# One more group's terms folded on GpSimd, and the routing steps of two groups one slot later

## The chip, the cores and the metric

The kernel runs on one core of a Trainium2 chip. The metric is the device time of one execution in microseconds (us), the median of several runs. TensorE is called PE here, VectorE DVE, ScalarE ACT, GpSimd POOL and SyncE SP in the rows of the profile; each works through its own list of instructions in order, and semaphores are the only thing that ties one list to another.

## The reference

```python
def xattn(k, v, q, ssm_kernel, D, head_dim):          # called with ctx, ctx, layernorm(x)
    kv = jnp.einsum('bhil,bhjl->bijhl', k_, v_)        # k_, v_, q_: [16, 16 heads, 8, 256]
    y = causal_convolution(kv, ssm_kernel)             # written with an FFT of 512
    out = y + kv * D[None, None, None, :, None]
    return jnp.einsum('bijhl,bhil->bjhl', out, q_)     # reshaped to [16, 128, 256]

def moe(x, Wg, W1, W3, W2, sw1, sw3, sw2):             # x: 2048 tokens of 256, E = 8, C = 256
    probs = softmax(xt @ Wg); eidx = argmax(probs); gate = probs[eidx]
    pos = (jnp.cumsum(oh, axis=0) * oh).sum(-1) - 1    # place of a token in its expert's list
    keep = pos < C
    xd = zeros(E * C, d).at[flat].set(xt, mode='drop')
    h = silu(xd @ W1) * (xd @ W3)                      # hidden size 352, per expert
    out = take(h @ W2, flat) * (gate * keep)[:, None]
    shared = silu(xt @ sw1) * (xt @ sw3) @ sw2
    return out + shared

x = x + tanh(g_xattn[0]) * xattn(ctx, ctx, layernorm(x))
x = x + tanh(g_ffn[0]) * moe(layernorm(x))
```

## The kernel before, in words

The 16 batches are worked on in 4 groups (g = 0 to 3) of 4 batches. A group's convolutions take 8 *slots*, one for each pair of heads, so slots 0 to 31 (CONV = 32) hold the convolutions, and slots 32 to 50 the rest of the shared feed-forward; the eight experts follow. Slot s of group g is s = 8g + i. The code is written out by hand: every engine runs `for s in range(SLOTS)`, and the table STEPS says in which slot of the next group a step of group g is due (`due(step, s)`); THIRD_STEPS and LAST_STEPS replace it for groups 2 and 3. Within a slot each engine's order is that of the code.

- GpSimd makes kv, the products of the context (L442 and L445, `kv_products`), eight slots ahead, one for every second slot, in a ring of 5. PE convolves them with Toeplitz matrices (L1097, L1100, `convolve`) into the PSUM tile z, of which there are two: the convolution of slot s waits for VectorE's products of slot s - 2.
- VectorE multiplies z with the queries qr (L461, `products`, six instructions a slot) into `terms`, 8 rows of terms that are still to be summed.
- `turn_r` (L1125) of a group turns and sums them on PE: one transpose for each term that accumulates in PSUM, so 4 x 8 = 32 transposes in each of its two halves. For groups from FULL_TERMS on, GpSimd first adds rows 4 to 7 to rows 0 to 3 (`fold`, L614, one call a slot, issued one slot after the products, behind the kv product of that slot), and PE turns 4 rows, 16 transposes a half. VectorE adds the result to x (L876, `first_residual`, two halves).
- The norms: VectorE's statistics (L842, L845, L847, L848, `norm_stats`), GpSimd's power and bias (L586, L587), ScalarE's normalised rows (L691). ln1 gives the queries of the next group but one (xn), ln2 the tokens (xrow).
- `turn_q(g)` (L1112) turns the normalised x of group g in two halves; ScalarE copies them into qr (L721, L726). `turn_xT(g)` (L1137) turns the tokens xrow.
- The routing: `logits(g)` turns the router's results (L1149); `choose(g)` on VectorE (L893 to L910) finds the expert, the one-hot rows and the running counts; ScalarE takes the exponential (L741). `places(g)` on PE (L1160, L1162) counts the tokens ahead of each; `slot_of_token(g)` on VectorE (L929 to L934) reads them, `gate(g)` follows (L915 to L921), and GpSimd scatters the token rows to memory (L619).
- The shared feed-forward is spread over the slots by SHARED_AT: ("gu", n, c) is 12 matmuls (L1188) with silu on ScalarE (L758) and a product on VectorE (L945), ("y", n, 0) is 12 matmuls (L1212) with L950 on VectorE. gu(0,0) stands in slot 21, gu(0,1) in slot 22.
- The weights of the shared feed-forward are split into a high and a low part in slot 12; GpSimd (L627) and VectorE (L986) make a half of the low part each.

All turns and the routing share two PSUM tiles tp0 and tp1 in strict turn. The list TP (`transposing_uses`) numbers the uses; use n takes tp[n % 2] and waits (`tp_wait`) until use n - 2 has been read:

```python
def tp_wait(eng, n):
    if n >= 2:
        by_act = BY_ACT[TP[n - 2][0]]
        count = sum(BY_ACT[TP[k][0]] == by_act for k in range(n - 1))
        eng.wait_ge(tp_free_act if by_act else tp_free_dve, count)
```

In the part that the change touches, the uses are (before) 10 r(1) half 0, 11 logits(0), 12 r(1) half 1, 13 places(0), 14 and 15 the two halves of q(3), 16 and 17 xT(1).

Of the kernel before, what the change touches and what calls it, by code (L numbers as in the profile page):

```python
# [69 lines left out]
REST_SLOT = 21  # L70
TERMS = 8
TURNS = 50
FULL_TERMS = 2
HEADS = 24
TROW = HEADS * 64
EXPERT_SPLIT_SLOT = CONV + 12
# [4 lines left out]
STEPS = {  # L81
    "ln1_stats": 1, "ln1_scale": 2, "ln1_apply": 2, "turn_q": 5,
    "turn_r0": 1, "turn_r1": 2, "residual0": 2, "residual1": 3, "ln2_stats": 3, "ln2_scale": 4, "ln2_apply": 5,
    "turn_xT": 6, "tokens_low": 7, "logits": 10, "exp": 10, "places": 12, "gate": 12, "scatter": 12,
}
THIRD_STEPS = {"ln2_apply": -4, "logits": 1, "exp": 1, "places": 2, "gate": 2, "scatter": 2}
LAST_STEPS = {
# [7 lines left out]
def due(step, s):  # L95

    if step in PREPARING:
        g, late = divmod(s - STEPS[step], UNITS)
        return g + 1 if late == 0 and 0 < g + 1 < NG else -1
    if s == CONV + LAST_STEPS[step]:  # L100
        return NG - 1
    if step in THIRD_STEPS and s == CONV + THIRD_STEPS[step]:
        return NG - 2
    g, late = divmod(s - STEPS[step] - UNITS, UNITS)
    return g if late == 0 and 0 <= g < (NG - 2 if step in THIRD_STEPS else NG - 1) else -1
# [8 lines left out]
def unit(s):  # L114

    g, i = divmod(s, UNITS)
    return g, (i + 4 * (g % 2)) % UNITS
# [12 lines left out]
def terms_of(g):  # L130

    return TERMS if g < FULL_TERMS else TERMS // 2

# [51 lines left out]
def transposing_uses():  # L185

    uses = [("q", 0, 0), ("q", 0, 1)]
    for s in range(SLOTS):
        for what, step, parts in (("logits", "logits", (0,)), ("r", "turn_r0", (0,)), ("r", "turn_r1", (1,)), ("q", "turn_q", (0, 1)),
                                  ("xT", "turn_xT", (0, 1)), ("pos", "places", (0,))):  # L190
            if due(step, s) >= 0:
                uses += [(what, due(step, s), k) for k in parts]
    uses += [("xe", e, 0) for e in range(E)]
    return uses


TP = transposing_uses()
TP_AT = {use: n for n, use in enumerate(TP)}
BY_ACT = {"q": True, "xT": False, "xe": False, "r": False, "logits": False, "pos": False}


def build(nc, x, ctxt, kpad, skip_d, g_x, g_f, wg, w1, w3, w2, sw1, sw3, sw2, out):
# [4 lines left out]
    with ExitStack() as ctx:  # L207
# [229 lines left out]
        def kv_products(eng, g, i, first, done):  # L437

            n = 4 - first
            dst, left = kv_planes(g, i, 64 * first, 0, [[64, n], [1, 64]], [[0, n], [1, 64]])  # L440
            _, right = kv_planes(g, i, 0, PL * first, [], [[PL, n], [1, 64]])
            eng.tensor_tensor(dst, left, right, ALU.mult)  # L442
            dst, left = kv_planes(g, i, 256, 0, [[1, 32]], [[1, 32]])
            _, right = kv_planes(g, i, 0, 32, [], [[1, 32]])
            eng.tensor_tensor(dst, left, right, ALU.mult).then_inc(done, 1)  # L445
# [127 lines left out]
        def _(pool):  # L573
# [35 lines left out]
            def fold(s):  # L609
                g, u = unit(s)  # L610
                pool.wait_ge(prods, s + 1)
                low, high = (view(terms, first_head(g, u) * 64 + i * 4 * TROW, [[TROW, 4], [1, 128]])
                             for i in range(2))
                pool.tensor_tensor(low, low, high, ALU.add).then_inc(folded, 1)  # L614
# [15 lines left out]
            for s in range(SLOTS):  # L630
                g, i = kv_due(s)
                if g >= 0:
                    kv_place_free(pool, g, i)
                    kv_products(pool, g, i, 1, kv_pool)
                if 1 <= s <= CONV and unit(s - 1)[0] >= FULL_TERMS:
                    fold(s - 1)
# [440 lines left out]
        def _(pe):  # L1077
            def convolve(s):

                g, u = unit(s)  # L1080
                i = s % UNITS // 2
                if g == 0 and i == 0:
                    pe.wait_ge(kv_dve, 1)
                else:
                    pe.wait_ge(kv_pool, 4 * g + i)
                    pe.wait_ge(kv_square, 4 * g + i)
                if s == 0:
                    pe.wait_ge(diag_added, 2)
                elif g == 0 and (s == 1 or u % 2 == 0):
                    pe.wait_ge(toep_in[u // 2], 16)  # L1090
                if s >= 2:
                    pe.wait_ge(prods, s - 1)
                for k in range(2):
                    h = 2 * u + k
                    o = (4 * g + i) % KVRING * KVQ + h % 4 * KVH

                    pe.matmul(view(z[s % 2], k * 512 + GB, [[PL, NPL], [1, GB]]), toep[:, h, P:2 * P],  # L1097
                              view(kv, o, [[PL, NPL], [1, GB]]), start=True, stop=False,
                              skip_group_check=True)
                    mm = pe.matmul(z[s % 2][:, k, 0:KVH], toep[:, h, 0:P], view(kv, o, [[1, KVH]]),  # L1100
                                   start=False, stop=True, skip_group_check=True)
                mm.then_inc(z_ready, 1)
# [12 lines left out]
            def turn_r(g, k):  # L1115
                pe.wait_ge(prods, UNITS * (g + 1))
                if g >= FULL_TERMS:
                    pe.wait_ge(folded, UNITS * (g + 1 - FULL_TERMS))
                n = TP_AT[("r", g, k)]
                tp_wait(pe, n)  # L1120
                for j in range(2 * BLK):
                    b, blk = 2 * k + j // BLK, j % BLK
                    for t in range(terms_of(g)):
                        src = view(terms, t * TROW + first_head(g, 0) * 64 + blk * GB + b, [[PL, CH]])
                        mm = pe.matmul(tp[n % 2][:, j * P:(j + 1) * P], src, ident[:, :], is_transpose=True,  # L1125
                                       start=(t == 0), stop=(t == terms_of(g) - 1))
                mm.then_inc(tp_ready, 1)
# [16 lines left out]
            def logits(g):  # L1144
                n = TP_AT[("logits", g, 0)]
                tp_wait(pe, n)
                pe.wait_ge(lg_copied, 2 * (g + 1))
                for b in range(GB):
                    mm = pe.transpose(tp[n % 2][:, b * E:(b + 1) * E], lgT[:, b * P:(b + 1) * P], ident[0:E, 0:E])  # L1149
                mm.then_inc(tp_ready, 1)  # L1150
# [66 lines left out]
            def turn_xe(e):  # L1217
                n = TP_AT[("xe", e, 0)]
                tp_wait(pe, n)
                pe.wait_ge(xe_in[e % XRING], 16 * (e // XRING + 1))  # L1220
                for k in range(2):
                    for t in range(2):
                        mm = pe.transpose(tp[n % 2][:, k * CAP + t * P:k * CAP + (t + 1) * P],  # L1223
                                          xe[:, e % XRING, t, k * P:(k + 1) * P], ident[:, :])
                mm.then_inc(tp_ready, 1)
# [7 lines left out]
            for s in range(SLOTS):  # L1233
                if 1 <= s < CONV:
                    convolve(s)
                if s in SHARED_AT:
                    feed_forward(FU_AT[SHARED_AT[s]])
                if due("logits", s) >= 0:
                    logits(due("logits", s))
                for k in range(2):  # L1240
                    if due(f"turn_r{k}", s) >= 0:
                        turn_r(due(f"turn_r{k}", s), k)
                for step, work in (("turn_q", turn_q), ("turn_xT", turn_xT), ("places", places)):
                    if due(step, s) >= 0:
                        work(due(step, s))
                if s >= XE_SLOT:
                    turn_xe(s - XE_SLOT)
# [36 lines left out]
```

## Time and profile before

| | |
|---|---|
| median of 3 runs | 219.16 us (218.25 to 421.25) |
| profiled execution | 219.47 us, of which 217.7 us are the span |
| PE busy | 201.6 us (93% of the span) |
| DVE, POOL, ACT busy | 148.4, 125.1, 80.7 us |
| granted TensorE clock, mean | 0.993 of full speed |

The span runs from the first to the last instruction. Busy shares are means over stages that differ: the convolutions with their products take the first half, the experts the second. What a step is worth is read from the stretch it stands in, in order of time, and from who waits for whom there. The ends of matmuls are modelled, so the distance from one start to the next says how long PE was held.

### The profile page before, as it was taken

How to read it: one execution, taken by the hardware profiler on the slowest of the kernel's cores; microseconds unless marked ns; L12 is line 12 of the kernel's file. 1: busy time of each engine (PE TensorE's matmuls, PEld its weight loads, DVE VectorE, ACT ScalarE, POOL GpSimd, SP SyncE). 2: the span in 40 equal slices, each digit the busy share in tenths (PEclk: the TensorE clock that was granted, in tenths of full speed). 3: DMA queues.
4: the chain of work that ended last, by engine and by line, in shares of the span. 5: the costliest groups of instructions: out<-in, count | busy, mean ns of one | idle time of the engine just before them, and what ended most of it. 6: DMA issues, size and time to landing. Idle time of an engine off the chain costs nothing.

```text
span 217.7 us, 4054 instructions
## 1 busy us (share of the span) xinstructions
PE 201.6 (93%) x1395; PEld 184.6 (85%) x1395; DVE 148.4 (68%) x488; ACT 80.7 (37%) x152; POOL 125.1 (57%) x129
## 2 busy tenths in 40 slices
PE   5978999969999999999999998999999999999970
PEld 5856789758998989898989998999999999999950
DVE  4678898699788987589867847353755775567230
ACT  2334412471653551322336237223354245423200
POOL 4399937486854599614682270540085587775751
PEclk9999999999999999999999999999999999999997
DMA  3789995000000010010201899833537669422221
GB/s 111 280 212 350 368 402 231 0 0 2 6 0 0 3 49 17 34 50 0 97 3 49 280 357 354 296 88 94 168 98 236 228 224 312 133 62 92 71 67 48
DMA packets 21926, 29.77 MB, mean 137 GB/s; under 512 B 3263, under 2 KB 19399, under 8 KB 21905
## 3 DMA queue, kind: packets, MB, share of 16 engines
q1 hardware_dynamic: 19248, 22.65, 31.7%
q0 software_dynamic: 2304, 6.05, 8.4%
q10 hardware_dynamic: 352, 0.81, 1.2%
q8 instruction: 11, 0.18, 0.4%
q14 instruction: 11, 0.08, 0.1%
HBM read 21.32 MB, written 8.45 MB: 137 GB/s over the span
## 4 chain that ended last, share of the span: by engine, by line
PE 76%; POOL 6%; DVE 4%; DMA 4%; issue 4%; ACT 2%; POOLq 1%; ACTq 1%; DVEq 0%
PE fb L1188 16%; PE z L1188 13%; PE z L1212 12%; PE tp L1125 10%; PE z L1100 9%; PE fb L1212 6%; PE z L1097 5%; POOL kv L442 4%; DMA ct<-ctxt 4%; DVE terms L461 2%; PE tp L1223 2%; POOL kv L445 1%; PE tp L1137 1%; DVE wl_gu L986 1%; ACT xrow L691 1%
## 5 line engine op out<-in xcount | busy, mean ns | idle before, releaser
L461 DVE TENSOR_TENSOR terms<-z,qr 128x512 f32<-128x512 f32 (+2 forms) x192 | 48.9, 326 | 7.3 <-PE z L1100 7.2
L1100 PE MATMUL z<-kv,toep 128*128 128x288 f32 x128 | 41.5, 406 | 0.0
L442 POOL TENSOR_TENSOR kv<-ct 128x768 f32<-128x768 f32 x15 | 28.3, 1884 | 13.9 <-PE z L1100 8.3
L668 POOL DMA_INDIRECT kv<-out,tok x16 | 22.3, 1392 | 18.2 <-DMA out<-x_sb 13.6
L1188 PE MATMUL fb<-xTh,wh_gu 128*128 128x256 f32 (+1 forms) x104 | 32.3, 311 | 0.2 <-issue 0.2
L1097 PEld LDWEIGHTS z<-kv,toep 128*128 128x128 f32 x128 | 22.2, 190 | 10.9 <-issue 7.0
L1097 PE MATMUL z<-kv,toep 128*128 128x144 f32 x128 | 26.8, 291 | 4.1 <-DMA toep<-kskip_scratch 2.3
L1188 PE MATMUL fb<-xTl,wh_gu 128*128 128x256 f32 (+1 forms) x104 | 29.0, 279 | 0.0
L1188 PE MATMUL fb<-xTh,wl_gu 128*128 128x256 f32 (+1 forms) x104 | 29.0, 279 | 0.0
L614 POOL TENSOR_TENSOR terms<-terms 128x512 f32<-128x512 f32 x16 | 20.3, 1286 | 11.1 <-DVE terms L461 11.1
L619 POOL DMA_INDIRECT xd_scratch<-xrow,dest x16 | 16.1, 1003 | 17.4 <-DVE xrow L921 7.3
L1188 PE MATMUL z<-xTh,wh_gu 128*128 128x256 f32 (+1 forms) x88 | 25.7, 292 | 0.0
L1188 PE MATMUL z<-xTl,wh_gu 128*128 128x256 f32 (+1 forms) x88 | 24.4, 278 | 0.0
L1188 PE MATMUL z<-xTh,wl_gu 128*128 128x256 f32 (+1 forms) x88 | 24.4, 277 | 0.0
L679 POOL DMA_INDIRECT out<-kv,tok x16 | 16.1, 1007 | 12.8 <-DVE kv L962 8.2
L1125 PE MATMUL tp<-ident,terms 128*128 128x128 f32 x192 | 23.0, 277 | 0.0
L1125 PEld LDWEIGHTS tp<-ident,terms 128*128 128x128 f32 x192 | 22.2, 193 | 0.3
L758 ACT ACTIVATE sg<-fb 128x256 f32<-128x256 f32 (+1 forms) x26 | 9.8, 376 | 31.4 <-PE fb L1188 29.5
L1188 PEld LDWEIGHTS fb<-xTh,wh_gu 128*128 128x128 f32 (+1 forms) x104 | 19.3, 186 | 1.3 <-issue 0.6
L1100 PEld LDWEIGHTS z<-kv,toep 128*128 128x128 f32 x128 | 20.0, 190 | 0.0
L1188 PEld LDWEIGHTS fb<-xTh,wl_gu 128*128 128x128 f32 (+1 forms) x104 | 19.3, 186 | 0.7
L1188 PEld LDWEIGHTS fb<-xTl,wh_gu 128*128 128x128 f32 (+1 forms) x104 | 19.3, 185 | 0.0
(132 smaller groups left out, 389.5 us busy)
## 6 DMA issues: line engine op xcount, KB each, us to landing
terms<-w SPq DMA_DIRECT2D x16, 352.0 KB, 8.3
ct<-ctxt SPq DMA_DIRECT2D x3, 768.0 KB, 8.5
xd_scratch<-xrow SPq DMA_DIRECT2D x4, 516.0 KB, 9.9
kv<-xd_scratch SPq DMA_DIRECT2D x8, 258.0 KB, 5.1
out<-x_sb SPq DMA_DIRECT2D x8, 256.0 KB
terms<-w SPq DMA_DIRECT2D x8, 256.0 KB, 8.3
x_sb<-x SPq DMA_DIRECT2D x3, 512.0 KB, 6.5
toep<-kskip_scratch SPq DMA_DIRECT2D x3, 512.0 KB, 8.0
```

The costliest lines, as they stand in the source:

```text
L442: eng.tensor_tensor(dst, left, right, ALU.mult)
L461: return eng.tensor_tensor(view(terms, t0 + row * TROW + col, [[64, 2], *td]), view(src, zo, [[512, 2], *zd]), view(qr, q0 + qo, [[CW, 2], ...
L614: pool.tensor_tensor(low, low, high, ALU.add).then_inc(folded, 1)
L619: pool.indirect_dma_start(out=xd, out_offset=bass.IndirectOffsetOnAxis(ap=dest[:, n:n + 1], axis=0), in_=xrow[:, g % 2, b, :], in_offset=N ...
L668: pool.indirect_dma_start(out=bg[:, e % BRING, t, :], out_offset=None, in_=out_rows, in_offset=bass.IndirectOffsetOnAxis(ap=tok[:, e, t:t ...
L679: pool.indirect_dma_start(out=out_rows, out_offset=bass.IndirectOffsetOnAxis(ap=tok[:, e, t:t + 1], axis=0), in_=fin[:, e % 2, t, :], in_o ...
L758: act.activation(sg[0:n, k % SGS, :], bank[0:n, 0:256], ACT.Silu).then_inc(silu_done, 1)
L1097: pe.matmul(view(z[s % 2], k * 512 + GB, [[PL, NPL], [1, GB]]), toep[:, h, P:2 * P], view(kv, o, [[PL, NPL], [1, GB]]), start=True, stop=F ...
L1100: mm = pe.matmul(z[s % 2][:, k, 0:KVH], toep[:, h, 0:P], view(kv, o, [[1, KVH]]), start=False, stop=True, skip_group_check=True)
L1125: mm = pe.matmul(tp[n % 2][:, j * P:(j + 1) * P], src, ident[:, :], is_transpose=True, start=(t == 0), stop=(t == terms_of(g) - 1))
L1188: mm = pe.matmul(bank[0:rows(blk, c), m * 256:(m + 1) * 256], wt[w % 2][:, col:col + rows(blk, c)], xt[:, place, k, first:first + 256], st ...
L1212: mm = pe.matmul(bank[:, t * L:(t + 1) * L], hidden(blk, c)[0:rows(blk, c), t * P:(t + 1) * P], down[0:rows(blk, c), c * L:(c + 1) * L], s ...
```

## The change

Three edits. FULL_TERMS goes from 2 to 1, so that group 1's terms are folded by GpSimd too (slots 9 to 16) and its turn_r takes 16 transposes a half instead of 32. logits and exp of groups 0 and 1 go from step 10 to 11, places, gate and scatter from 12 to 13 (slots 18 to 19 and 20 to 21 for group 0; 26 to 27 and 28 to 29 for group 1). And places stands ahead of turn_q within a slot, which matters in slot 21, where places(0) and turn_q(3) now meet. The list TP follows: 10 and 11 r(1), 12 logits(0), 13 places(0), 14 and 15 q(3).

```diff
--- before.py
+++ after.py
@@ -70,7 +70,7 @@
 REST_SLOT = 21
 TERMS = 8
 TURNS = 50
-FULL_TERMS = 2
+FULL_TERMS = 1
 HEADS = 24
 TROW = HEADS * 64
 EXPERT_SPLIT_SLOT = CONV + 12
@@ -81,7 +81,7 @@
 STEPS = {
     "ln1_stats": 1, "ln1_scale": 2, "ln1_apply": 2, "turn_q": 5,
     "turn_r0": 1, "turn_r1": 2, "residual0": 2, "residual1": 3, "ln2_stats": 3, "ln2_scale": 4, "ln2_apply": 5,
-    "turn_xT": 6, "tokens_low": 7, "logits": 10, "exp": 10, "places": 12, "gate": 12, "scatter": 12,
+    "turn_xT": 6, "tokens_low": 7, "logits": 11, "exp": 11, "places": 13, "gate": 13, "scatter": 13,
 }
 THIRD_STEPS = {"ln2_apply": -4, "logits": 1, "exp": 1, "places": 2, "gate": 2, "scatter": 2}
 LAST_STEPS = {
@@ -186,8 +186,8 @@
 
     uses = [("q", 0, 0), ("q", 0, 1)]
     for s in range(SLOTS):
-        for what, step, parts in (("logits", "logits", (0,)), ("r", "turn_r0", (0,)), ("r", "turn_r1", (1,)), ("q", "turn_q", (0, 1)),
-                                  ("xT", "turn_xT", (0, 1)), ("pos", "places", (0,))):
+        for what, step, parts in (("logits", "logits", (0,)), ("r", "turn_r0", (0,)), ("r", "turn_r1", (1,)), ("pos", "places", (0,)),
+                                  ("q", "turn_q", (0, 1)), ("xT", "turn_xT", (0, 1))):
             if due(step, s) >= 0:
                 uses += [(what, due(step, s), k) for k in parts]
     uses += [("xe", e, 0) for e in range(E)]
@@ -1240,7 +1240,7 @@
                 for k in range(2):
                     if due(f"turn_r{k}", s) >= 0:
                         turn_r(due(f"turn_r{k}", s), k)
-                for step, work in (("turn_q", turn_q), ("turn_xT", turn_xT), ("places", places)):
+                for step, work in (("places", places), ("turn_q", turn_q), ("turn_xT", turn_xT)):
                     if due(step, s) >= 0:
                         work(due(step, s))
                 if s >= XE_SLOT:
```

PE from the second half of group 1's turn_r to the convolution of slot 22; tp0 and tp1 are the shared PSUM tiles, z0 and z1 the convolution's. Before, slots 18 to 20:

```order
L1149 MATMUL tp1<-ident,lgT 128x8 x3
L1125 MATMUL tp0<-ident,terms 128x128 [waits tp_free_dve,prods]
L1125 MATMUL tp0<-ident,terms 128x128 x31
L1097 MATMUL z1<-kv,toep 128x36x4 [waits prods,kv_square,kv_pool]
...
L1160 MATMUL tp1<-oh,tri 128x32 [waits pool_consts,onehot,tp_free_dve]
L1162 MATMUL tp1<-acc,ones 128x32
L1097 MATMUL z1<-kv,toep 128x36x4 [waits prods,kv_square,kv_pool]
```

Now, slots 18, 21 and 22:

```order
L1125 MATMUL tp1<-ident,terms 128x128 [waits tp_free_dve,folded,prods]
L1125 MATMUL tp1<-ident,terms 128x128 x15
...
L1160 MATMUL tp1<-oh,tri 128x32 [waits pool_consts,onehot,tp_free_dve]
L1162 MATMUL tp1<-acc,ones 128x32
L1112 MATMUL tp0<-ident,xn 128x128 [waits tp_free_dve,xn_done]
L1112 MATMUL tp0<-ident,xn 128x128 x3
L1112 MATMUL tp1<-ident,xn 128x128 [waits tp_free_dve]
L1112 MATMUL tp1<-ident,xn 128x128 x3
L1097 MATMUL z0<-kv,toep 128x36x4 [waits prods,kv_square,kv_pool]
```

turn_r waits for the folds too and is half as long; places(0) has moved from slot 20 to right in front of turn_q(3), whose second half takes the tile that places(0) has used, and the convolution of slot 22 is behind both.

VectorE around the first reader of the places, L929. Before, its place is behind the products of slot 20:

```order
L461 TENSOR_TENSOR terms<-z,qr 128x2x3x40
L461 TENSOR_TENSOR terms<-z,qr 128x2x24
L461 TENSOR_TENSOR terms<-z,qr 128x2x2x16
L461 TENSOR_TENSOR terms<-z,qr 128x2x2x8
L929 TENSOR_TENSOR t<-tp,oh 128x32 [waits tp_ready]
L931 TENSOR_REDUCE slotf<-t 128x4 [waits tp_free_dve]
```

Now (t2 and tp1 are the same with their buffer numbers), behind the products of slots 20 and 21 and L945:

```order
L461 TENSOR_TENSOR terms<-z0,qr 128x2x2x8
L461 TENSOR_TENSOR terms<-z1,qr 128x2x4x64 [waits q_done,z_ready]
L461 TENSOR_TENSOR terms<-z1,qr 128x128
L461 TENSOR_TENSOR terms<-z1,qr 128x2x3x40
L461 TENSOR_TENSOR terms<-z1,qr 128x2x24
L461 TENSOR_TENSOR terms<-z1,qr 128x2x2x16
L461 TENSOR_TENSOR terms<-z1,qr 128x2x2x8
L945 TENSOR_TENSOR hT<-fb0,sg 128x256 [waits silu_done]
L929 TENSOR_TENSOR t2<-tp1,oh 128x32 [waits tp_ready]
```

One slot's products and an L945 have come in front of L929.

GpSimd from its half of the weight split in slot 12 to slot 16. Before:

```order
L627 TENSOR_TENSOR wl_gu0<-shared_gu,wh_gu0 128x768
L442 TENSOR_TENSOR kv<-ct 128x4x192
L445 TENSOR_TENSOR kv<-ct 128x4x32
L442 TENSOR_TENSOR kv<-ct 128x4x192
L445 TENSOR_TENSOR kv<-ct 128x4x32
L614 TENSOR_TENSOR terms<-terms 128x4x128
```

Now:

```order
L627 TENSOR_TENSOR wl_gu0<-shared_gu,wh_gu0 128x768
L614 TENSOR_TENSOR terms<-terms 128x4x128
L442 TENSOR_TENSOR kv<-ct 128x4x192
L445 TENSOR_TENSOR kv<-ct 128x4x32
L614 TENSOR_TENSOR terms<-terms 128x4x128 x2
L442 TENSOR_TENSOR kv<-ct 128x4x192
L445 TENSOR_TENSOR kv<-ct 128x4x32
L614 TENSOR_TENSOR terms<-terms 128x4x128 x2
```

Four folds (slots 12 to 15) stand between the split and the last of group 1; the last row's second fold is that of slot 16, which the kernel before has as well.

## Rows read from the trace of the kernel before

**Rows 1.** Busy time by stretch: PE, PEld, DVE, ACT, POOL, each with its count

```profile
27.40:40.50 13.10, 13.08 (x97) 12.18 (x98) 10.05 (x36) 4.17 (x7) 5.63 (x6) 1.00 0.65 258
81.00:111.00 30.00, 29.78 (x200) 26.86 (x199) 23.00 (x89) 8.78 (x17) 17.96 (x19) 1.00 0.10 36
```

**Rows 2.** The chain that ended last, 71 to 78 us: start, duration, what

```profile
71.40 1.42 PE fb L1188 x12
...
73.36 1.17 ACT qr L721 x2
...
75.09 2.07 ACT xrow L691 x4
...
77.21 1.09 PE tp L1137 x8
```

**Rows 3.** PE in order of time: start, duration, instruction

```profile
57.12 3.74 PE L1125 MATMUL tp<-ident,terms 128*128 128x128 f32 x32
60.70 0.41 PE L1097 MATMUL z<-kv,toep 128*128 128x144 f32 x2
...
67.75 0.41 PE L1097 MATMUL z<-kv,toep 128*128 128x144 f32 x2
...
69.21 0.30 PE L1160 MATMUL tp<-oh,tri 128*128 128x32 f32 x2
...
73.72 0.41 PE L1097 MATMUL z<-kv,toep 128*128 128x144 f32 x2
...
86.77 1.97 PE L1125 MATMUL tp<-ident,terms 128*128 128x128 f32 x16
88.57 0.41 PE L1097 MATMUL z<-kv,toep 128*128 128x144 f32 x2
```

**Rows 4.** PE's weight loads at 73 us: in brackets the idle time before

```profile
73.23 0.42 PEld L1112 LDWEIGHTS tp<-ident,xn 128*128 128x128 f32 x4 [0.21 <-DVE t L929]
```

**Rows 5.** DVE in order of time, slots 18 to 21, and one of POOL

```profile
62.42 1.55 DVE L461 TENSOR_TENSOR terms<-z,qr 128x512 f32<-128x512 f32 x6 [0.77 <-PE z L1100]
...
64.32 1.05 DVE L896 SCALAR_TENSOR_TENSOR t<-sh,prio 128x32 f32<-128x32 f32 x1
...
66.93 0.75 DVE L876 SCALAR_TENSOR_TENSOR x_sb<-tp,tg,x_sb 128x512 f32<-128x512 f32 x1
68.01 1.55 DVE L461 TENSOR_TENSOR terms<-z,qr 128x512 f32<-128x512 f32 x6 [0.33 <-PE z L1100]
...
73.00 0.17 DVE L929 TENSOR_TENSOR t<-tp,oh 128x32 f32<-128x32 f32 x1
...
74.35 1.54 DVE L461 TENSOR_TENSOR terms<-z,qr 128x512 f32<-128x512 f32 x6
75.81 0.42 DVE L945 TENSOR_TENSOR hT<-fb,sg 128x256 f32<-128x256 f32 x1
...
64.04 1.28 POOL L614 TENSOR_TENSOR terms<-terms 128x512 f32<-128x512 f32 x1 [1.91 <-DVE terms L461]
```

**Rows 6.** POOL in order of time, slots 12 to 14

```profile
45.63 1.82 POOL L627 TENSOR_TENSOR wl_gu<-shared_gu,wh_gu 128x768 fp32r<-128x768 f32 x1
...
49.91 0.45 POOL L445 TENSOR_TENSOR kv<-ct 128x128 f32<-128x128 f32 x1
```

**Rows 7.** Single lines: duration in ns, least/median/most; first and last start

```profile
L614 POOL TENSOR_TENSOR terms<-terms x16: 1266/1284/1311, 55.4 to 112.2; 128x512 f32<-128x512 f32 x16
...
L847 DVE TENSOR_SCALAR veps<-mv x8: 170/171/996, 6.3 to 121.7; 128x4 f32<-128x4 f32 x8
...
L896 DVE SCALAR_TENSOR_TENSOR t<-sh,prio x4: 191/194/1046, 64.3 to 132.9; 128x32 f32<-128x32 f32 x4
...
L442 POOL TENSOR_TENSOR kv<-ct x15: 1810/1842/2546, 10.2 to 79.2; 128x768 f32<-128x768 f32 x15
```

**Rows 8.** POOL and DVE at 122 us, in order of time

```profile
122.01 1.04 POOL L586 TENSOR_TENSOR rstd<-veps,mhalf 128x4 f32<-128x4 f32 x1 [6.10 <-DVE mneg L848]
...
122.61 0.16 DVE L932 TENSOR_TENSOR mine<-mine,slotf 128x4 f32<-128x4 f32 x1
```

## The prediction

> **What bounds the kernel now.** The busy time by stretches comes first: from 81 to 111 us PE works 29.78 of 30.00 us, VectorE 23.00 [rows 1], so PE work that goes away is worth its time wherever PE is what everyone waits for. The change works between 28 and 62 us on GpSimd and between 57 and 110 us on PE and VectorE, so the second view is the chain of waits around its middle. It runs along PE except at one place: PE's turning of the next queries (L1112, turn_q) goes through ScalarE's copies (L721) and ScalarE's normalised rows (L691) to PE's turn_xT at 77.21 [rows 2]. The third view, PE in order of time, gives the sizes: the 32 transposes of a first-half turn_r start at 57.12 and the next convolution at 60.70, so they hold PE for 3.58 us; the same call of group 2, with 16, goes from 86.77 to 88.57, 1.80 us. A slot's convolution takes 1.46 us (67.75 to 69.21) [rows 3]. The fourth, the weight loads, shows the detail that decides: the second half of turn_q was ready at 73.0 and waited for VectorE's L929, the first reader of the places [rows 4]. Both use the PSUM tile tp1, which L929 sets free. The fifth, VectorE from 62 to 76 us, is almost without gaps: 0.77 us before the products at 62.42, 0.33 us at 68.01, no more until L929 at 73.00 [rows 5]. So in slots 18 to 21 VectorE is as good as the bound.
>
> **What is removed.** 2 x 16 transposes of group 1: 2 x (3.58 - 1.80) = 3.6 us of PE [rows 3]. If all of it came through, the kernel would end 3.6 us earlier.
>
> **GpSimd's folds.** Eight more of 1.28 us, 10.3 us in all [rows 7]. Up to slot 12 they cost nothing: four fit into GpSimd's idle time, which is 7.5 us of the 13.1 between 27.40 and 40.50 [rows 1]. What counts is fold(15), for which turn_r of group 1 now waits. Followed from GpSimd's half of the weight split at 45.63, which I put 0.2 us later because the statistics ahead of it meet a fold: split until 47.65; VectorE's half of the split (L986) had to wait for it and then ran an estimated 0.8 us, while the next kv product stood still (2.55 us, the longest of all, instead of 1.84) [rows 6, 7], so fold(12) ends at 48.45 + 1.28 = 49.7; kv product 1.84 + 0.45 less their overlap, 2.25, to 51.95; folds 13 and 14 to 54.45; kv product to 56.7; fold(15) to 57.95. PE would be there at 57.12 + 0.25 [rows 3]. The wait is 0.6 us, and the whole turn ends about 1 us earlier than before, not 1.8. The trace has no fold in these slots. Bounds: none, if GpSimd gains 0.6 us in the eight slots; 1.9 us, if each of the eight is held up once by 0.16 us.
>
> **Places and queries.** This is the part that costs. In slot 21 PE now issues gu(0,0), then places(0), then turn_q(3), then the convolution of slot 22. places needs the one-hot rows of choose(0), which VectorE now does in slot 19, behind two products and the ln2 statistics. And the second half of turn_q waits, as it did before, for L929. But L929 has moved from behind the products of slot 20 to behind the products of slot 21 and the L945 that follows. Its new time, from VectorE's own queue between 62.42 and 73.00 [rows 5]:
> - added ahead of it: one slot's products, 1.46 us (1.54 less the overlap with the next), and L945, 0.33 us: +1.8.
> - choose(0) no longer meets a fold. In the trace its L896 took 1.05 us, beside a median of 0.19 over the four groups [rows 7], and ended with GpSimd's fold, begun at 64.04 and 1.28 us long [rows 5, 7]: -0.86.
> - the gap of 0.77 us before products(18) closes, because PE comes earlier; that of 0.33 at 68.01 becomes about 0.6, since the second residual is done at 64.15 and the convolution of slot 19 only at 64.75 (58.05 + 1.8 + 1.46 + 1.8 + 1.46, and 0.2 to the start): -0.5.
> - the small L847 of the statistics waits for what GpSimd is doing (0.17 us alone, up to 1.00 [rows 7]). For ln1(3) a kv product now stands in its way for some 0.3 us, for ln2(1) fold(19) (67.45 to 68.7) for some 0.6: +0.9. Bounds: 0, and 2 x 0.83 = 1.66.
> Sum +1.3: L929 starts at 74.35. The same as a walk: residual 61.2, products(18) 61.95 to 63.4, residual to 64.15, products(19) 64.75 to 66.2, statistics to 68.85, choose(0) to 71.05, products(20) to 72.5, products(21) to 74.0, L945 to 74.35. From there everything is as before: from 73.00 to the convolution of slot 22 it was 0.72 us [rows 3, 5], and to turn_xT 4.21 us, through L721, L726 and L691 [rows 2, 5]. So slot 22's convolution starts at 75.1, the gu product behind it (1.42) is through at 78.0, and turn_xT, which needs the rows, starts at 78.55 instead of 77.21. PE has by then stood still for 0.6 us at the fold, 1.4 before places (from 69.3, which is 63.1 and three convolutions, the logits' 0.4 and gu(0,0), to 70.7, 1.8 us into choose), 3.1 inside turn_q and 0.6 before turn_xT; that is more than the 3.6 us of transposes and the little it stood still before.
>
> **Group 1's logits and places** (slots 27 and 29) cost nothing. VectorE is idle for 7 of the 30 us around them [rows 1]. choose takes it about 2.2 us (from the end of the products at 62.42 to 66.93, less the 0.86 of the stall [rows 5]); this now lies ahead of products(28), for which the convolution of slot 30 waits, two slots later. The cover is the gap that PE's longer slots (1.46 of convolution and 1.42 or more of other matmuls against 1.46 of products) leave, an estimated 0.7 us; without it PE would wait for the difference, at most 2.2. Scatter(0) and scatter(1) start later, but their readers come 6 us or more after. The folds of group 2 are done some 4 us before turn_r of group 2 asks for them.
>
> **What is late next.** From slot 23 on PE has no wait to absorb anything, and every later load or gather is released by PE or what follows it, so the 1.35 us reaches the end whole. The profiled execution is 219.47 us, 1.8 us over its span and 0.3 above the median of 219.16. 219.47 + 1.35 = 220.8; for the median 219.16 + 1.35 = 220.5.
>
> **A rule weighed.** The Trainium skill, "SBUF — State Buffer", "Who interferes with whom" and "Terms", has VectorE and GpSimd share a port pair that whoever starts first holds for its whole instruction. The L896 and L847 rows agree. By it GpSimd's L586, which follows the statistics, should also hold up L896 of the moved choose.
>
> **Rivals.**
> - L586 blocks choose(0): L586 would run from 68.9 to 69.9, L896 would start at 69.3 and lose 0.6 us, so L929 is at 74.95: 221.1. Against it: at 122.01 to 123.05 L586 ran while VectorE's L932, with two SBUF inputs, took its usual 0.16 us [rows 8]. The page named above would have had it wait until 123.05. The same holds for choose(1), within its 0.7 us of cover. Chance 0.1.
> - Even: no fold wait and no L847 collisions. L929 shifts by 1.8 - 0.86 - 1.1 = -0.2 to +0.4. Time 219.2. For it: GpSimd's order of instructions against VectorE's is uncertain by more than one fold. Chance 0.22.
> - The order doesn't bite: something frees tp1 early, or the chain through ScalarE is the only limit. Then turn_q ends at 71.5, VectorE's products(20) (72.6) release the convolution, turn_xT starts at 75.65, and 1.6 us is gained: 217.6. Against it: the wait shows in the weight loads [rows 4]. Chance 0.1. That the removed 3.6 us come through whole (215.6) would need VectorE to be idle there; 0.03.
> - Slower by GpSimd: it falls behind in slots 13 to 16 and fold(15) comes late. Up to 57.4 it costs nothing; from there each us shifts turn_r, the products of slots 18 and 19 and L929 by nearly as much, since little VectorE slack is left. Fold(15) at 60 us gives L929 at 76.3 and 222.5. For it: eight folds (10.3 us) and five kv products (11.3 us) in 24 us. Chance 0.13, 0.03 of it beyond 4.4 us.
> - That the folds don't take place: excluded, the order of instructions has eight more L614.
>
> **How the numbers follow.** Forecast (0.42): 220.5, its own range 219.8 to 221.3. Slower by over 2% (4.4 us, about what a measurement of this kernel can tell from no change): 0.04. Faster by over 2%: 0.02. Within: 0.94. The range takes in the even case and GpSimd's delay to 222.2, and leaves out the gain: 218.6 to 222.2.
>
> **What the new profile would show.** L614 x24; L1125 x160; turn_r of group 1 waiting 0.6 us for L614; PE idle before L1160 and, for some 3 us, in the weight loads of L1112 with L929 as releaser; the convolution of slot 22 near 75. Wrong if L929 starts before 73 us, if PE waits anew after slot 23, or if L461 itself becomes slower beside the folds.

## The result: slower by 1.65%, more than twice the forecast shift

The median went from 219.12 to 222.54 us (221.30 to 222.94); the ratio is 1.0165, 95% interval 1.0138 to 1.0192, so 3.0 to 4.2 us. Here and below, ratios leave out executions more than 1.5% slower than the fastest of the same kernel, which medians and ranges keep. The forecast was +1.35 us, and its range ended at 222.2 us. The profiled execution took 222.49 us with a span of 220.8, that is 3.1 us more span than before; the sums below are made against it.

The page of the changed kernel, spans and busy times:

```profile
span 220.8 us, 3998 instructions
PE 200.4 (91%) x1363; PEld 182.6 (83%) x1363; DVE 149.2 (68%) x488; ACT 80.6 (36%) x152; POOL 135.1 (61%) x137
...
PEclk9999999999999889999999999999999999999995
```

GpSimd is busy for 10 us more, as the eight new folds ask for. PE has lost only 1.2 us of busy time although 32 transposes are gone. The row of the clock has two 8s, at 72 to 83 us, where the kernel before had 9s.

PE in order of time around the change (start, duration, instruction, idle time before it and its releaser), the answer to [rows 3]:

```profile
57.83 2.04 PE L1125 MATMUL tp<-ident,terms 128*128 128x128 f32 x16 [0.30 <-issue]
59.70 0.41 PE L1097 MATMUL z<-kv,toep 128*128 128x144 f32 x2
...
61.16 1.93 PE L1125 MATMUL tp<-ident,terms 128*128 128x128 f32 x16
...
67.05 0.48 PE L1097 MATMUL z<-kv,toep 128*128 128x144 f32 x2 [0.50 <-DVE terms L461]
...
71.20 0.38 PE L1160 MATMUL tp<-oh,tri 128*128 128x32 f32 x2 [1.08 <-issue]
...
71.64 0.64 PE L1112 MATMUL tp<-ident,xn 128*128 128x128 f32 x4
75.15 0.70 PE L1112 MATMUL tp<-ident,xn 128*128 128x128 f32 x4 [2.87 <-DVE t L929]
75.64 0.69 PE L1097 MATMUL z<-kv,toep 128*128 128x144 f32 x2
76.12 1.16 PE L1100 MATMUL z<-kv,toep 128*128 128x288 f32 x2
...
80.15 1.04 PE L1137 MATMUL tp<-ident,xrow 128*128 128x128 f32 x8
...
89.66 1.97 PE L1125 MATMUL tp<-ident,terms 128*128 128x128 f32 x16
```

Read it against [rows 3]. A half of turn_r(1) now holds PE for 1.8 us in place of 3.6. PE stands still four times: 0.30 us before the first half, until just after fold(15) has ended (57.7; the row names no releaser), 0.50 before the convolution of slot 21, 1.08 before the places, and 2.87 in the middle of turn_q. Then come matmuls that take nearly twice as long: the pair at 76.12 takes 1.16 us, and slot 22's convolution lasts from 75.64 to about 78.5, about 2.9 us in place of 1.46. turn_xT starts at 80.15; before, at 77.21 [rows 2]. From there to turn_r(2) it is 9.5 us in both kernels (89.66 here, 86.77 before), and the difference of 2.9 us stays to the end (3.1 us in the spans).

The stretches of 1 or 2 us of the changed kernel there (busy PE, PEld, DVE, ACT, POOL, and behind them the granted clock):

```profile
74.00:75.00 1.00, 0.00 (x0) 0.00 (x0) 1.00 (x7) 0.00 (x0) 0.68 (x2) 1.00 0.00 0
75.00:76.00 1.00, 0.85 (x6) 0.85 (x7) 0.86 (x7) 0.12 (x1) 0.00 (x0) 0.82 0.00 0
76.00:78.00 2.00, 2.00 (x7) 1.60 (x6) 0.33 (x2) 1.97 (x4) 0.63 (x1) 0.50 0.00 0
78.00:80.00 2.00, 2.00 (x13) 1.81 (x12) 1.24 (x5) 1.11 (x3) 1.68 (x3) 0.74 0.19 66
80.00:82.00 2.00, 2.00 (x17) 1.90 (x16) 1.17 (x5) 1.65 (x4) 2.00 (x2) 1.00 0.19 66
```

PE was granted half speed (1.2 of 2.4 GHz) from shortly before 76 until 79 us (the stretch 78:80 averages it with full speed), right behind its standstill of 2.87 us.

VectorE in order of time, the answer to [rows 5], with four rows of GpSimd and one of ScalarE below:

```profile
60.76 0.43 DVE L847 TENSOR_SCALAR veps<-mv 128x4 f32<-128x4 f32 x1
61.11 1.32 DVE L848 TENSOR_SCALAR mneg<-mv 128x4 f32<-128x4 f32 x1
...
65.36 1.55 DVE L461 TENSOR_TENSOR terms<-z,qr 128x512 f32<-128x512 f32 x6
...
68.66 0.82 DVE L847 TENSOR_SCALAR veps<-mv 128x4 f32<-128x4 f32 x1
...
69.91 0.19 DVE L896 SCALAR_TENSOR_TENSOR t<-sh,prio 128x32 f32<-128x32 f32 x1
...
71.66 3.00 DVE L461 TENSOR_TENSOR terms<-z,qr 128x512 f32<-128x512 f32 x12
74.57 0.42 DVE L945 TENSOR_TENSOR hT<-fb,sg 128x256 f32<-128x256 f32 x1
74.90 0.19 DVE L929 TENSOR_TENSOR t<-tp,oh 128x32 f32<-128x32 f32 x1
...
56.44 2.54 POOL L614 TENSOR_TENSOR terms<-terms 128x512 f32<-128x512 f32 x2
...
61.14 1.27 POOL L614 TENSOR_TENSOR terms<-terms 128x512 f32<-128x512 f32 x1
...
68.16 1.29 POOL L614 TENSOR_TENSOR terms<-terms 128x512 f32<-128x512 f32 x1
69.63 1.02 POOL L586 TENSOR_TENSOR rstd<-veps,mhalf 128x4 f32<-128x4 f32 x1 [0.18 <-DVE mneg L848]
...
77.05 2.07 ACT L691 ACTIVATE xrow<-x_sb,nbias,rstd 128x256 f32<-128x256 f32 x4
```

L929, which the forecast had at 74.35, starts at 74.90. The small L848 ran until 62.43, when the fold begun at 61.14 was over, and L847 at 68.66 until the fold of 68.16 was. L896 took its 0.19 us although L586 ran beside it. The token rows were ready at 79.12, but PE took up turn_xT only at 80.15, because it was still working, slowly, on what stood ahead.

### The profile page after: what moved, and what is told of

It is laid out like the page before. It is cut to its first block, busy times and chain, and to the rows that moved or that the text cites. A ratio compares the mean times of both kernels' runs of the same rounds, so it can differ in the third digit from the quotient of the medians.

```text
span 220.8 us, 3998 instructions
## 1 busy us (share of the span) xinstructions
PE 200.4 (91%) x1363; PEld 182.6 (83%) x1363; DVE 149.2 (68%) x488; ACT 80.6 (36%) x152; POOL 135.1 (61%) x137
## 4 chain that ended last, share of the span: by engine, by line
PE 73%; DVE 9%; POOL 6%; issue 4%; DMA 4%; ACT 1%; POOLq 1%; ACTq 1%; DVEq 0%
PE fb L1188 15%; PE z L1188 13%; PE z L1212 12%; PE z L1100 9%; PE tp L1125 8%; PE fb L1212 6%; PE z L1097 5%; POOL kv L442 4%; DVE terms L461 4%; DMA ct<-ctxt 4%; PE tp L1223 2%; POOL kv L445 1%; DVE stats L842 1%; PE tp L1137 1%; DVE wl_gu L986 1%
## 5 line engine op out<-in xcount | busy, mean ns | idle before, releaser
L1100 PE MATMUL z<-kv,toep 128*128 128x288 f32 x128 | 42.5, 415 | 0.0
L614 POOL TENSOR_TENSOR terms<-terms 128x512 f32<-128x512 f32 x24 | 31.2, 1314 | 14.1 <-DVE terms L461 14.1
L1097 PEld LDWEIGHTS z<-kv,toep 128*128 128x128 f32 x128 | 22.6, 194 | 12.2 <-issue 7.6
L1097 PE MATMUL z<-kv,toep 128*128 128x144 f32 x128 | 27.6, 298 | 4.8 <-DVE terms L461 2.5
L442 POOL TENSOR_TENSOR kv<-ct 128x768 f32<-128x768 f32 x15 | 27.5, 1832 | 6.1 <-DMA ct<-ctxt 5.8
L1100 PEld LDWEIGHTS z<-kv,toep 128*128 128x128 f32 x128 | 20.5, 194 | 0.0
L1125 PE MATMUL tp<-ident,terms 128*128 128x128 f32 x160 | 19.2, 276 | 0.3 <-issue 0.3
L1125 PEld LDWEIGHTS tp<-ident,terms 128*128 128x128 f32 x160 | 18.7, 193 | 0.9 <-issue 0.5
```

## The experiments

Each kernel was run against the kernel before on the same chip; ratios are to that. "D" is the distance in the trace from the start of slot 18's convolution to turn_xT. It is used because the times of two traces differ by up to 2 us before the change has any effect. In the changed kernel D is 80.15 - 59.70 = 20.45 us, in the kernel before 77.21 - 60.70 = 16.51 us [rows 2, 3]; the first half of turn_r(1) lies ahead of D, so what it saves isn't in it. Where an experiment adds lines to the kernel, the line numbers behind them are higher by 2 or 4: L1112 is L1114 or L1116 there, L929 is L931, L848 is L850.

**1. The folds alone.** The kernel before with

```diff
-FULL_TERMS = 2
+FULL_TERMS = 1
```

> Only FULL_TERMS = 1; logits, exp, places, gate and scatter stay in their old slots and places stays behind turn_q. Theory A (the loss is the reader of the places, L929, behind one more slot of VectorE's work, and the clock that PE loses in the wait): L929 near 73.3, no wait of more than 0.5 us inside turn_q, turn_xT near 77.5, the median within 1 us of the kernel before, 218.7 to 220. Theory B (GpSimd's folds are the loss: turn_r waits for them and they hold up VectorE's small instructions, wherever the routing steps stand): the whole loss stays, 222 to 223.

Measured: 220.2 us, ratio 1.0048 (1.0004 to 1.0092). Six of the ten executions took 218.6 to 220.7 us and four took 222.1 to 223.4. PE in order of time in the profiled one, which is the fastest (where the second half of turn_r(1) starts, then turn_xT), and three stretches around the first:

```profile
61.97 3.14 PE L1125 MATMUL tp<-ident,terms 128*128 128x128 f32 x16 [1.53 <-DVE x_sb L876]
...
76.39 1.09 PE L1137 MATMUL tp<-ident,xrow 128*128 128x128 f32 x8 [0.48 <-ACT xrow L691]
...
60.00:62.00 2.00, 0.47 (x6) 0.38 (x5) 1.97 (x3) 0.00 (x0) 1.89 (x2) 1.00 0.00 0
62.00:64.00 2.00, 2.00 (x12) 2.00 (x13) 1.93 (x9) 1.41 (x3) 0.99 (x3) 0.66 0.00 0
64.00:66.00 2.00, 2.00 (x10) 1.86 (x9) 1.83 (x9) 1.97 (x4) 0.76 (x1) 0.50 0.00 0
```

With the routing where it was, there is no wait in turn_q. The 3.6 us of transposes are gone and the median does not fall; the profiled execution has 0.8 us less span than the kernel before. PE waits 1.53 us for L876, which came late behind an L848 of 1.31 us beside a fold; then its 16 transposes take 3.14 us, most of it at half clock, in place of 1.9. Most of what the folds give, VectorE's queue and the clock take. The four above 222 us lost as much as the change does, at the same mean clocks (0.982 to 0.988 in all ten). None of them has a trace, so it stays open what held them up.

**2. The later routing alone.** The changed kernel with `FULL_TERMS = 2`, so without the new folds.

> FULL_TERMS stays 2, so no fold in group 1; the routing steps are one slot later and places ahead of turn_q. Theory A: the 3.6 us of transposes are back on PE and the late reader too: VectorE's products(20), products(21) and L945 follow a choose(0) that ends near 73.4, L929 near 76.7, PE stands still for over 2 us inside turn_q, the convolution of slot 22 runs at half the clock; 223 to 224.5. Theory B: with no folds there is nothing to lose, 218.5 to 220.

Measured: 223.79 us, ratio 1.0199 (1.0141 to 1.0257). PE at the second half of turn_q:

```profile
76.16 1.12 PE L1112 MATMUL tp<-ident,xn 128*128 128x128 f32 x4 [2.87 <-DVE t L929]
```

The same standstill, the same half clock behind it, and turn_xT at 80.97 (D 20.77). This part alone, without the new folds, brings the whole loss; the folds alone brought as much only in the four untraced executions of experiment 1.

**3. The queries' turn ahead of the places.** The changed kernel, with PE's code and the list TP in the old order:

```diff
-for step, work in (("places", places), ("turn_q", turn_q), ("turn_xT", turn_xT)):
+for step, work in (("turn_q", turn_q), ("turn_xT", turn_xT), ("places", places)):
```

> The changed kernel, but places again behind turn_q and turn_xT within a slot (code and tile order). Theory A: the second half of turn_q waits for logits(0) alone, which are long read; the next limit is products(20), near 73.2, and the rows of ScalarE near 76.1; turn_xT near 76.2 instead of 80.15; about 4 us less than the changed kernel, 217.6 to 219. Theory B: as the changed kernel, 222 to 223.

Measured: 218.47 us, ratio 0.9981 (0.9948 to 1.0014). PE:

```profile
69.23 1.04 PE L1112 MATMUL tp<-ident,xn 128*128 128x128 f32 x8
71.89 0.41 PE L1160 MATMUL tp<-oh,tri 128*128 128x32 f32 x2 [1.63 <-ACT qr L721]
```

Both halves of turn_q now run as one, D is 16.64 us, and the whole loss of 1.65% is gone. So it hangs on the order of places and turn_q in the two tiles. PE stands still here too, for 1.63 us; the seven executions with a mean clock of 0.988 and more took 217.8 to 218.8 us, the three with 0.981 to 0.983 took 219.2 to 219.8. GpSimd's last fold for turn_r(2), and turn_r(2) itself:

```profile
81.25 3.77 POOL L614 TENSOR_TENSOR terms<-terms 128x512 f32<-128x512 f32 x3
...
85.12 2.02 PE L1125 MATMUL tp<-ident,terms 128*128 128x128 f32 x16
```

The fold ends at 85.02, 0.1 us before PE takes it up; in the changed kernel it ended at 85.80 and PE came at 89.66. With its 4 us given back, PE is as early as GpSimd allows. Experiment 8 depends on this.

**4. The standstill filled.** The changed kernel, with transposes of the identity into a free tile between the halves of turn_q(3); nothing of the result uses them, and VectorE's queue is as it was:

```diff
+if g == NG - 1 and k == 1:
+    pe.wait_ge(f_free, 2)
+    for _ in range(22):
+        pe.transpose(fb[1][:, 0:P], ident[:, :], ident[:, :])
```

> The changed kernel with 22 transposes of a constant into a free PSUM bank between the halves of turn_q(3), where PE stands still for 2.9 us; they take an estimated 2.5 us at the rate of turn_r and are over before L929. If the standing still is what halves the clock: granted clock 1.00 from 75 to 80 us, the convolution of slot 22 in 1.5 us instead of 2.9, turn_xT at 79.2, when its rows are ready, so 1.0 us less, 221.5. If the clock falls for another reason, or its fall costs nothing: 222.5.

Measured: 221.47 us, ratio 1.0076 (1.0041 to 1.0111). PE:

```profile
71.64 2.57 PE L1113 MATMUL fb<-ident 128*128 128x128 f32 x22
...
74.67 0.66 PE L1116 MATMUL tp<-ident,xn 128*128 128x128 f32 x4 [0.47 <-DVE t L929]
...
78.65 1.09 PE L1141 MATMUL tp<-ident,xrow 128*128 128x128 f32 x8 [0.47 <-ACT xrow L691]
```

The second half still waits for L929, but PE is not idle meanwhile. From the second half to turn_xT it is 3.98 us, where the changed kernel needs 5.00, and turn_xT waits again for the rows of ScalarE, as before the change [rows 2]. The clock was 1.00 from 70 to 80 us. That is 1.0 us less, and the median is 1.1 us lower: this is the clock's share of the loss. The ratios differ by 0.9%, or 1.9 us, and are uncertain by 1.0.

**5. The standstill alone.** The kernel before, with nothing changed but a wait of turn_q's second half for the products of slot 21:

```diff
+if g == NG - 1 and k == 1:
+    pe.wait_ge(prods, 22)
```

> The kernel before with one wait added: the second half of turn_q(3) waits for VectorE's products(21), which end near 75.9 instead of L929 at 73.2. No fold, nothing else moved. PE stands still for 2.8 us. If a stop of that length halves the clock by itself: granted clock 0.5 for some 3 us after it, the convolution of slot 22 in 2.9 us, turn_xT at 80.9 instead of 77.2, 222.8. If it doesn't: convolution in 1.5 us, turn_xT at 79.9, 221.8.

Measured: 222.78 us, ratio 1.0161 (1.0122 to 1.0201). A standstill of this length at this place costs 1.6% without any fold or moved routing step. That it is the very loss of the change is partly luck: this kernel keeps the 3.6 us of transposes and has none of the new stalls of VectorE. PE and its stretch behind:

```profile
75.75 0.69 PE L1114 MATMUL tp<-ident,xn 128*128 128x128 f32 x4 [2.69 <-DVE terms L461]
...
76.00:78.00 2.00, 2.00 (x10) 1.71 (x9) 0.03 (x1) 1.49 (x3) 1.68 (x3) 0.56 0.19 66
```

**6. The norm's scale ahead of the fold on GpSimd**, in slots 18 and 20 (`fold(s - 1)` moved behind the scales), to get the fold out of the way of L847 and L848. First in the changed kernel:

> The changed kernel; in slots 18 and 20 alone GpSimd does the norm's power and bias ahead of the fold, so that no fold can start beside VectorE's L847 and L848. If those stalls (L848 1.32 us instead of 0.16, L847 0.82 instead of 0.17) delay L929: L848 back at 0.16, L929 some 1.3 us earlier, 73.6, the standing still in turn_q unchanged at about 2.9 us because choose(0) moves with it, the clock still halved: 221.2 to 221.6. If the stalls are hidden: 222.5.

Measured: 221.94 us, ratio 1.0123 (1.0085 to 1.0165). L848 takes 0.16 us, but now `acc<-acc,pair` (L908) in choose takes 1.24 beside the moved fold. Counted from slot 18's convolution, the second half of turn_q starts at 75.11 - 59.95 = 15.16 us, in the changed kernel at 75.15 - 59.70 = 15.45: 0.3 us sooner, where 1.3 was expected. The same edit with the queries first:

> queries_first with the same order on GpSimd as scale_first. With the stalls as a cause: choose(0) and products(20) some 1.2 us earlier, PE waits less before L1160; ScalarE's rows depend on the statistics too: turn_xT 0.5 to 1.2 us earlier, 217.3 to 218. If the stalls are hidden: as queries_first, 218.5.

Measured: 218.76 us (217.3 to 219.9), ratio 0.9978 (0.9946 to 1.0010); against 0.9981 without the edit, nothing. In the profiled execution something was gained and lost again. The places start at 70.26 - 58.64 = 11.62 us from slot 18's convolution, 1.4 us sooner than in experiment 3 (71.89 - 58.85 = 13.04). But PE stands still 0.99 us before them and 1.12 us behind them, the clock is 0.50 from 74 to 76 us, and D is 17.73 against 16.64. And with the folds alone of experiment 1:

> folds_only with GpSimd's power and bias ahead of the fold in slots 18 and 20. With the stalls as a cause: L848 0.16 instead of 1.31, so the first residual frees its tile 1.2 us earlier, PE's stop of 1.5 us before the second half of turn_r shrinks to 0.4, the clock stays at 1.00 there, turn_xT near 75; 217 to 217.8. If hidden: as folds_only, 219 to 220.

Measured: 221.9 us, ratio 1.0125 (1.0095 to 1.0155): a clear miss. VectorE within choose(0), and PE's next convolution:

```profile
64.03 1.30 DVE L898 SCALAR_TENSOR_TENSOR t<-sh,prio 128x32 f32<-128x32 f32 x1
...
65.90 1.81 DVE L906 TENSOR_TENSOR pair<-oh 128x8 f32<-128x8 f32 x1
...
71.24 0.82 PE L1099 MATMUL z<-kv,toep 128*128 128x144 f32 x2 [2.34 <-DVE terms L461]
```

One instruction met a fold (62.77 to 65.29) and another a kv product (65.88 to 67.69). PE then stood 2.34 us for VectorE's products; the clock had fallen before it went on, and was 0.50 from 71 to 74 us. Reordering GpSimd moved the stalls; it didn't remove them. The folds without the later routing can thus lose 1.25% by themselves, if they meet other instructions; its six executions took 221.4 to 222.4 us, nearly as long as the four above 222 us of experiment 1.

**7. The folds of slots 17 to 19 postponed** behind that of slot 20, all in slot 21:

```diff
-if 1 <= s <= CONV and unit(s - 1)[0] >= FULL_TERMS:
+if 1 <= s <= CONV and unit(s - 1)[0] >= FULL_TERMS and s not in (18, 19, 20):
     fold(s - 1)
+    for late in ((17, 18, 19) if s == 21 else ()):
+        fold(late)
```

> The changed kernel, but GpSimd's folds of slots 17, 18 and 19 are issued in slot 21, behind fold(20), so that none runs beside choose(0) and the normalisation of VectorE; their results are used only later. If GpSimd's folds lengthen VectorE's small instructions, the mneg and rstd instructions take 0.16 and 0.17 us in place of 1.32 and 0.82, nothing in choose takes over 1 us for that reason, and the start of the logits' instruction on VectorE comes about 1.2 us earlier, near 73.7 us. The standstill within turn_q and the halved clock behind it stay, since they come from the reader's place: 221.3 us. If these stalls were hidden beside TensorE's work, the time stays at 222.5.

Measured: 220.15 us, ratio 1.0055 (1.0031 to 1.0079), 1.1% under the change. Now the fold-free VectorE, and PE:

```profile
60.12 0.16 DVE L850 TENSOR_SCALAR mneg<-mv 128x4 f32<-128x4 f32 x1
...
66.97 0.17 DVE L849 TENSOR_SCALAR veps<-mv 128x4 f32<-128x4 f32 x1
...
72.57 0.18 DVE L931 TENSOR_TENSOR t<-tp,oh 128x32 f32<-128x32 f32 x1
...
72.81 1.12 PE L1114 MATMUL tp<-ident,xn 128*128 128x128 f32 x4 [2.87 <-DVE t L931]
```

Counted from slot 18's convolution, the second half of turn_q comes at 72.81 - 58.71 = 14.10 us, in the changed kernel at 75.15 - 59.70 = 15.45: the stalls cost 1.35 us, 0.15 more than expected. The standstill is again 2.87 us. In the profiled execution the clock was 0.50 from 72 to 78 us, longer than in the changed kernel, so that D is 20.22, and 1.1 of the 1.35 us went again. So the trace doesn't show where the 2.4 us between the two medians come from. That execution took 221.12 us, and the three with a mean clock under 0.98 took 221.1 to 221.8, the others 219.4 to 220.7.

**8. All together.** The queries first, with 12 transposes of the identity ahead of places(0); the queries first with postponed folds; and both with 8 transposes.

> The version with the next queries' turn ahead of the places, with 12 transposes of the identity (nothing of the result uses them) put into the TensorE program just ahead of places(0) in slot 21, where TensorE otherwise stands for about 1.6 us. If it is the standstill that lets the clock fall in some executions, the clock is 1.00 from 60 to 80 us in each execution, and all times lie near 218.1 us, about 1 us under the runs of the version without the transposes that showed a dip. If the fall has another cause, or costs nothing on the path, the times are spread as before round 218.5.

> The next queries' turn ahead of the places, and the folds of slots 17, 18 and 19 issued in slot 21. If both costs are real and apart from each other, neither the standstill within turn_q nor the stalls are left: 217.3 to 217.8 us. If the stalls only move to another of VectorE's instructions, as with the scales ahead of the folds: 218.5.

> As the version with the queries first and the folds postponed, with 8 transposes of the identity (nothing of the result uses them) ahead of places(0). If all three causes are as told, the clock is 1.00 throughout, and the time 217.0 to 217.6 us, under both kernels. If the clock's dip costs nothing there, it is the same as without the transposes.

| | median, us | ratio to before | D, us | turn_xT to turn_r(2), us |
|---|---|---|---|---|
| queries first, filled | 218.02 | 0.9951 (0.9931 to 0.9971) | 16.59 | 9.60 |
| queries first, postponed | 219.06 | 1.0025 (0.9994 to 1.0055) | 15.23 | 11.57 |
| both, filled | 219.88 | 1.0030 (1.0004 to 1.0056) | 15.24 | 11.57 |

The first is as expected, and the fastest of all: 0.5% under the kernel before. Against experiment 3 (0.9981) the transposes gain 0.3%, but the intervals overlap. Its clock was 1.00 from 56 to 84 us in the profiled execution, which all the same was its slowest: 219.36 us, with slot 18's convolution at 60.35, 1.5 us later than in experiment 3. Nearly all of that is there long before the change's stretch (a convolution released by a load of toep starts at 15.30, there at 13.89), so part of the spread has nothing to do with the clock. The other eleven took 217.6 to 218.9. The two with postponed folds missed. They reach turn_xT 1.35 us sooner, as expected, and lose 2.0 us on the way to turn_r(2). PE and GpSimd in the kernel of the second row, and PE in that of the third:

```profile
85.40 2.02 PE L1127 MATMUL tp<-ident,terms 128*128 128x128 f32 x16 [1.90 <-issue]
...
70.84 4.99 POOL L614 TENSOR_TENSOR terms<-terms 128x512 f32<-128x512 f32 x4 [2.36 <-DVE terms L461]
...
76.86 1.19 POOL L619 DMA_INDIRECT xd_scratch<-xrow,dest  x1 [0.92 <-POOL xrow L653]
...
79.36 1.86 POOL L442 TENSOR_TENSOR kv<-ct 128x768 f32<-128x768 f32 x1
...
81.57 3.73 POOL L614 TENSOR_TENSOR terms<-terms 128x512 f32<-128x512 f32 x3
```

```profile
85.86 3.23 PE L1127 MATMUL tp<-ident,terms 128*128 128x128 f32 x16 [1.86 <-issue]
```

GpSimd's three folds end at 85.30, and turn_r(2) starts 0.1 us later. The postponing isn't the main reason: counted from slot 18's convolution the folds end at 26.70 us, and at 26.17 in experiment 3, where PE took them up 0.1 us later too. So PE, now 1.35 us sooner, only waits 1.35 us longer for GpSimd, which was the limit there already, and another 0.5 us for the four folds in a row, behind which the scatters start later. Where the 1.9 us of standing still were followed by half clock (the 3.23 us of the last row), more was lost. That the clock falls there in most executions of these two kernels would fit their spread (218.3 to 221.4 us), but isn't shown: the times above 219.2 have mean clocks of 0.980 to 0.989, and so do three of 218.5 to 219.0.

## Why the prediction was wrong

The direction held, and the mechanism as far as L929: it comes late, turn_q waits for it through the tile tp1, and this costs more than the removed transposes give. A mechanism behind it was missing, and one size was off.

- **"From there everything is as before"** is the step that failed. The 4.2 us from L929 to turn_xT were taken from [rows 2 to 5], measured behind a PE that had hardly stood still. In the changed kernel they are 5.25 us. ScalarE kept to the old pace (rows ready 4.2 us after L929, at 79.12), but slot 22's convolution and the start of gu(0,1) ran at half clock behind the 2.87 us of standing still. I had forecast that standstill, at 3.1 us, and given it no price beyond its length. Experiment 4 takes out the clock's fall alone and measures 1.0 us; experiment 5 makes the standstill alone, and the half clock follows it again. The Trainium skill, "TensorE: Matmul & The Clock Gate", "HAM oscillation — how this bites in real kernels", tells of waits in mid-kernel after which the array starts again at the low clock. The rows at 76 us (0.50) agree that the array goes on at the low clock; the section's case is a wait for DMA that comes again in each round, and the price of this single one is from the rows alone.
- **The stalls of VectorE's small instructions**, +0.9 within 0 to 1.66: the two L847 took 0.43 and 0.82 us, so 0.9 between them, as forecast. L848 of the first norm took 1.32 in place of 0.16, which the sum did not have, because of these instructions it took L847 alone [rows 7]. The gap forecast before products(19) took in half of it: they start at 65.36 in place of 64.75, 0.6 us late, and L929 comes 0.55 us later than forecast. Experiment 7 puts all stalls together at 1.35 us, a size inside the bounds. Of the rule weighed in the prediction, [rows 7] shows durations of L847 only, not what GpSimd did beside it; the two above end with GpSimd's L445 (at 61.17) and with a fold.
- **What is left over.** 1.0 + 0.55 are 1.55 of the 1.75 us by which the profiled execution's span missed the forecast (3.1 against 1.35). The remaining 0.2 is not traced to a row. The median missed by 2.0 us; four runs do not fix it better than 0.6.
- **Right:** the removed transposes (1.8 us a half); fold(15) to end at 57.95 (57.70: the pair of folds from 56.44 has it first), with a wait of 0.3 us, not 0.6; no fold in choose(0), so L896 back to 0.19; PE idle before the places (1.08, forecast 1.4). Not forecast was the wait of 0.50 before slot 21's convolution.
- **Group 1 cost nothing,** as forecast: turn_r(2) at 89.66 and the end are both about 3 us late, like turn_xT, and places(1) at 107.55 waited for nothing.
- **Rivals.** L586 did not block choose: L896 at 69.91 ran within L586's 69.63 to 70.65. The Trainium skill, "SBUF — State Buffer", "Terms", would have had L896 wait for the whole of it; the row disagrees, while the L848 row, held until a fold's end, agrees. The even case and the slow GpSimd did not happen. "The order doesn't bite" was wrong for this kernel, but experiment 3, which removes the wait, shows that its 1.6 us of gain were too many as well: the ratio is 0.9981 there, or -0.4 us (-1.1 to +0.3).
- **The chances** gave the range's upper end, 222.2, to a slow GpSimd. The way that it really went, a forecast wait that slows the work behind it, was no rival, and it gave 222.5.

## What to carry to other kernels

When a change puts a wait of some microseconds on a busy PE, price the matmuls behind it at the lower clock too, and look whether the cause is only the order in which two steps take a shared tile: putting the step that others wait for first gave back all 1.65% here, and filling the 2.87 us in which PE was idle with unused transposes made that kernel faster (experiment 4). Before work is moved to GpSimd, list all of VectorE's small SBUF instructions beside it, not the one that was seen to stall; moving the fold only chose which of them waits (experiment 6). And before time is won on PE, look how much later than GpSimd it takes up what GpSimd hands it: here the slack was 3.9 us in the changed kernel and 0.1 us once the loss was undone, so what experiment 8 won ahead of that point could not come through.

## What the runs showed of the hardware

- The granted clock fell to 0.50 within or right behind every profiled standstill of 2.3 to 2.9 us of a PE otherwise over 90% busy (experiments 2, 5, 7, the first and third kernel of 6, and the change). With shorter ones it did so behind 1.53 us (1), 1.86 us (the last of 8) and two stops of 0.99 and 1.12 us close together (the second kernel of 6), but not behind 1.63 us (3) nor 1.90 us (the second row of 8), so the length of a stop did not settle it alone. It stayed low for 3 to 7 us, and matmul pairs of 0.65 us took 1.16.
- With 22 transposes of a constant in the stop of 2.87 us, 0.47 us of it were left, and the clock stayed at 1.00 (experiment 4).
- VectorE's instructions on 128x4 to 128x32 elements, 0.16 to 0.19 us alone, took up to 1.32 us beside GpSimd's fold (1.27 to 1.29) and 1.81 beside its kv product (1.81); an L847 that met the end of a kv product and then a fold took 1.67 (experiment 3). Beside GpSimd's power on 128x4 (L586, 1.02 us) they took 0.16 to 0.19.
